# First attention layer: the products with V stand two steps behind the scores in place of one, with a third buffer of probabilities

## The reference, cut to what matters

```python
S = jnp.einsum('hid,hjd->hij', K, Q) * SCALE
delta = idx[:, None] - idx[None, :]
decay = jnp.where(delta < 0, 0.0, -delta.astype(jnp.float32) ** ALPHA)
S = jnp.where(delta < 0, -jnp.inf, S) + decay
C = jax.nn.softmax(S, axis=-1)
attn = jnp.einsum('hij,hjd->hid', C, V)
attn = attn.reshape(B, H, T, HD).transpose(0, 2, 1, 3).reshape(B, T, D)
return attn @ o_w.T + o_b
```

## Time and profile before

| | |
|---|---|
| median of 3 runs | 1562.99 us (1561.16 to 1569.36) |
| time of the profiled execution | 1574.49 us |
| its span, first to last instruction | 1572.8 us |
| PE, DVE, ACT busy over the span | 90%, 76%, 66% |
| first layer's attention | from 94 us to 546 us of the span |
| second layer's attention | from about 743 us to about 1390 us |

### The profile page before, as it was taken

The page is one execution under the profiler, slowest core; times in us unless marked ns, Lnnn a source line. Parts: engine busy times, 40 slices in busy tenths (PEclk is TensorE's granted clock), DMA queues, the critical chain, the costliest instruction groups (busy, mean ns, idle before and its releaser), DMA issues.

```text
span 1572.8 us, 35125 instructions
## 1 busy us (share of the span) xinstructions
PE 1423.1 (90%) x13272; PEld 601.4 (38%) x13272; DVE 1198.0 (76%) x1592; ACT 1034.1 (66%) x2043; POOL 308.0 (20%) x367
## 2 busy tenths in 40 slices
PE   7978798898999999986999999999999999998988
PEld 5643333333333354441233233333333333246664
DVE  5568797898786044788999979997999789536665
ACT  2135576777688833231799979988999889954432
POOL 1300122000000032223500038101200130154134
PEclk9888999999999999996999999999999999999999
DMA  7521120101000003223100200000000000012453
GB/s 226 124 54 41 35 80 27 37 27 49 5 2 2 1 14 68 48 48 92 49 7 8 54 5 6 7 7 6 7 7 6 7 2 2 19 64 85 142 154 119
DMA packets 57611, 68.54 MB, mean 44 GB/s; under 512 B 10563, under 2 KB 53123, under 8 KB 56707
## 3 DMA queue, kind: packets, MB, share of 16 engines
q1 hardware_dynamic: 54379, 57.90, 13.7%
q0 software_dynamic: 3072, 8.39, 1.8%
HBM read 45.29 MB, written 26.74 MB: 46 GB/s over the span
## 4 chain that ended last, share of the span: by engine, by line
PE 41%; issue 30%; DVE 16%; POOL 7%; ACT 5%; DMA 1%; another core or an unknown queue 0%; SPq 0%; POOLq 0%; DVEq 0%; ACTq 0%
DVE mpart L1704 13%; PE psum L1211 9%; PE psum L1186 5%; PE psum L1155 4%; ACT probs L1451 3%; PE psum L1328 3%; PE psum L1254 3%; PE psum L1282 2%; PE psum L1263 2%; PE psum L1347 2%; PE psum L1105 2%; PE psum L1241 1%; PE psum L1131 1%; PE psum L1319 1%; POOL ffn_w L937 1%
## 5 line engine op out<-in xcount | busy, mean ns | idle before, releaser
L1704 DVE TENSOR_REDUCE mpart<-psum 128x2 f32<-128x1024 f32 (+2 forms) x832 | 913.5, 1157 | 100.4 <-PE psum L1155 83.2
L1451 ACT ACTIVATE probs<-psum 128x512 f32<-128x512 f32 (+3 forms) x1664 | 846.4, 572 | 171.2 <-PE psum L1186 92.6
L1211 PE MATMUL psum<-probs,v_region 128*17 128x256 f32 (+2 forms) x6144 | 495.2, 395 | 11.7 <-ACT out_sb L1466 7.9
L1155 PE MATMUL psum<-key_region,row_region 50*128 50x512 f16 (+3 forms) x1664 | 322.7, 379 | 59.4 <-DVE mpart L1704 49.5
L1186 PE MATMUL psum<-row_region,key_region 52*128 52x512 f16 (+3 forms) x1664 | 348.9, 378 | 15.6 <-ACT probs L1451 13.4
L1186 PEld LDWEIGHTS psum<-row_region,key_region 52*128 52x128 f16 x1664 | 97.6, 93 | 352.1 <-ACT probs L1451 294.9
L1211 PEld LDWEIGHTS psum<-probs,v_region 128*17 128x17 f32 x6144 | 102.7, 95 | 206.2 <-issue 103.5
L1155 PEld LDWEIGHTS psum<-key_region,row_region 50*128 50x128 f16 x1664 | 94.4, 93 | 163.4 <-DVE mpart L1704 98.1
L899 POOL TENSOR_SCALAR vare<-mv 128x4 f32<-128x4 f32 x16 | 3.7, 232 | 635.3 <-DVE mv L1623 631.9
L1486 ACT ACTIVATE probs<-psum,gate_s 128x512 f32<-128x512 f32 (+1 forms) x24 | 16.4, 683 | 70.4 <-PE psum L1254 70.4
L1002 POOL TENSOR_TENSOR key_region<-probs,key_region 128x512 f16<-128x512 f32 (+1 forms) x24 | 27.9, 1166 | 153.7 <-ACT key_region L1495 153.6
(11 more groups left out here) (179 smaller groups left out, 1371.8 us busy)
## 6 DMA issues: line engine op xcount, KB each, us to landing
parts<-key_region SPq DMA_DIRECT2D x32, 256.0 KB, 2.8
key_region<-parts SPq DMA_DIRECT2D x48, 128.0 KB, 4.3
row_region<-parts SPq DMA_DIRECT2D x192, 32.0 KB
sorted_x<-in_zero SPq DMA_DIRECT2D x46, 128.0 KB, 2.6
key_region<-sorted_x SPq DMA_DIRECT2D x46, 128.0 KB
sorted_y<-key_region SPq DMA_DIRECT2D x46, 128.0 KB
key_region<-in_wmod SPq DMA_DIRECT2D x2, 1536.0 KB, 12.6
x_sb<-in_x SPq DMA_DIRECT2D x4, 512.0 KB, 8.3
```

What stands on the lines that cost most here:

```text
L1155: mm = pe.matmul(bank(b + par)[:, 0:w], rows[at, g, hp, r * P:(r + 1) * P], keys[at, g * HP + hp, q * CH:q * CH + w], start=True, stop=not ...
L1211: mm = pe.matmul(psum[32 * h:32 * h + VW, SUM_BANK, lo:hi], v_sb[:, jt, g * HG + h, :], probs[:, (S0[y] + s) % 2, h, lo:hi], start=(jt == ...
L1451: nc.scalar.activation(probs[:, (S0[y] + s) % 2, 2 * hp + par, off:CH], psum[:, e % 3, off:CH], ACT.Exp, scale=SCALES[y]).then_inc(s_p, 1)
L1704: V.tensor_reduce(mpart[:, n % NG, at:at + 2, q:q + 1], psum[:, b:b + 2, 0:w], AX.X, ALU.max).then_inc(drained(*item)[0], 1)
```

## The change

In the first layer, `values` of step s - 2 stands beside the scores of step s, where that of step s - 1 stood (`LAG = (2, 1)`: two for the first layer, one for the second, which keeps its order). A third buffer of probabilities lies in `ffn_w` behind the first layer's gate weights. `exps` waits for the products of three steps ago in place of two. All that follows the end of a unit (`oc`, `ft`, `bt`, `oq`, `op`, `st`, `nm`, `ln`) stands one step later, and `lh` at the first step of the unit after. At the end of the layer two steps of products are left in place of one. The maximum blocks, `mt`, `place`, `rows` and all DMAs stay where they are.

```diff
+LAG = (2, 1)
...
-            m, j = (n, k - 1) if k else (n - 1, steps_of(y, n - 1) - 1 if n else 0)
+            lag = LAG[y]
+            m, j = (n, k - lag) if k >= lag or not n else (n - 1, steps_of(y, n - 1) + k - lag)
             out.append(("sc", y, s, n, k, 0))
             out += work[:first]
-            if s:
-                out.append(("pv", y, s - 1, m, j, 0))
-            if n and n % NG == 0 and k == 3:
+            if s >= lag:
+                out.append(("pv", y, s - lag, m, j, 0))
+            if n and n % NG == 0 and k == lag + 2:
                 out.append(("oq", y, n // NG - 1))
             out.append(("sc", y, s, n, k, 1))
             out += work[first:second]
-            if s:
-                out.append(("pv", y, s - 1, m, j, 1))
-            if s and k == 0:
+            if s >= lag:
+                out.append(("pv", y, s - lag, m, j, 1))
+            if n and k == lag - 1:
                 out.append(("oc", y, n - 1))
...
-            if k == 1 and n:
+            if k == lag and n:
                 out.append(("ft", y, n - 1))
...
-                if k == 7:
+                if k == 7 and y:
                     out.append(("lh", 2 * y + 1, i))
...
+            if not y and k == 0 and n % NG == 1 and n > NG:
+                out.append(("lh", 1, n // NG - 1))
...
-    out += [("pv", y, total - 1, NU - 1, steps_of(y, NU - 1) - 1, z) for z in range(2)] + [("oc", y, NU - 1)]
+    out += [("pv", y, s, NU - 1, steps_of(y, NU - 1) + s - total, z) for s in range(total - LAG[y], total) for z in range(2)]
+    out.append(("oc", y, NU - 1))
...
+        prob_bufs = [probs[:, b, :, :] for b in range(2)] + [ffn_w[:, 0, KD * F0:KD * F0 + HG * CH].rearrange("p (h t) -> p h t", h=HG)]
...
+        def probs_of(y, s):
+            return prob_bufs[(S0[1] + s) % 2 if y else s % (LAG[0] + 1)]
...
-                if S0[y] + s >= 2 and hp == 0:
-                    act.wait_ge(s_pv, S0[y] + s - 1)
+                if hp == 0 and (y or s > LAG[0]):
+                    act.wait_ge(s_pv, S0[y] + s - LAG[y])
```

More of the change, by code:

```diff
@@ L201, in attention_walk @@
                 i = n // NG - 1
-                if k == 2:
+                if k == lag + 1:
                     out.append(("bt", y, i))
-                if k == 3:
+                if k == lag + 2:
                     out.append(("op", y, i))
-                if k == 4:
+                if k == lag + 3:
                     out.append(("st", 2 * y + 1, i))
-                if k == 5:
+                if k == lag + 4:
                     out.append(("nm", 2 * y + 1, i))
-                if k == 6:
+                if k == lag + 5:
                     out.append(("ln", 2 * y + 1, i))
-                if k == 7:
+                if k == 7 and y:
                     out.append(("lh", 2 * y + 1, i))
@@ L1211, in values @@
                         mm = pe.matmul(psum[32 * h:32 * h + VW, SUM_BANK, lo:hi], v_sb[:, jt, g * HG + h, :],
-                                       probs[:, (S0[y] + s) % 2, h, lo:hi], start=(jt == 0),
+                                       probs_of(y, s)[:, h, lo:hi], start=(jt == 0),
                                        stop=(z == 1 and jt == steps_of(y, n) - 1))
@@ L1450, in exps @@
                     act.wait_ge(s_e, e + 1)
-                    nc.scalar.activation(probs[:, (S0[y] + s) % 2, 2 * hp + par, off:CH], psum[:, e % 3, off:CH],
+                    nc.scalar.activation(probs_of(y, s)[:, 2 * hp + par, off:CH], psum[:, e % 3, off:CH],
                                          ACT.Exp, scale=SCALES[y]).then_inc(s_p, 1)
```

## The result

| kernel | median (range), us | runs |
|---|---|---|
| before | 1563.03 (1561.16 to 1569.36) | 7 |
| changed | 1572.89 (1570.92 to 1576.38) | 7 |

The ratio on record is 1.0047 [1.0025, 1.007], some 7 us slower; the two medians themselves lie 9.9 us apart. The forecast was 1562.0, and its range ended at 1569. Two later series with the same code gave 1.0000 [0.9975, 1.0025] and 1.0042 [1.0009, 1.0074]. So there are two things to explain, a loss and its coming and going.

A forecast was written before the change was run, and what follows sets the result against it. With maximum blocks DVE was taken as the bound, PE just behind; in the last 50 us ACT alone. Terms -2.0 - 0.5 + 0.5 + 0.5 + 0.6 = -0.9 us from 1562.99 gave 1562.1, stated as 1562.0, range 1554 to 1569.

The forecast's parts named there:

- The two wait terms: First layer's products with V wait less for probabilities: -2.0 us with maximum blocks, -0.5 in the last 50 us.
- The term of -2.0: First layer's stretch with maximum blocks: half the 3.9 us wait for probabilities gained (0 to -3.9).
- Narrow steps and unit starts: First layer's 16 units: PE's work is only redistributed between narrow and wide steps, +0.5 us.
- the middle: Over 16 units, +0.5 us between 5.0 lost if DVE or ACT paces wide steps and 4.0 gained if PE does.
- The prediction's own sign of it: First layer: forecast wrong if the count or length of stretches at clock 0.50 changes by more than 10 us.
- The rival in which the clock falls: Three of sixteen units fall to 1.2 GHz after two light opening steps: +9.3 us, 1572.3; chance 0.07.
- The end of the layer: After the first layer's last scores, one more half step of products on PE: +0.6 us (0.2 to 0.6).
- `lh`: Two ACT operations of 1.15 us move from a narrow step to unit 5's first wide one: +0.5 us.
- The third buffer: Third buffer of probabilities, with POOL writing the gate weights beside it: 0 us.

The follow-up runs named there:

- the fourth: Fourth series: the changed kernel without any addition, run a third time, against the kernel before: 1572.1 us for 1566.15, ratio 1.0042.
- The two splits: Kernel before with three buffers and lag 2 only in units 0 to 3 (ratios 1.004, 1.0036) or only in units 4 to 15 (1.000, 1.0008).
- the third series: The changed kernel without any addition, run once more against the kernel before: 1574.29 us, ratio 1.0000.

## Why the prediction was wrong, point by point

**The two wait terms (-2.0 and -0.5).** Their sum of -2.5 lies near the traces, -2.1 us in units 4 to 15, but not by the reasons given, and with an interval that holds 0 at equal time at the low clock. With maximum blocks DVE holds the step: its usual 2.23 us are the same in both kernels (units 13 and 14, step by step). The term of -2.0 is therefore not confirmed as a wait that was filled. For the last 50 us the prediction said "ACT alone is the bound there" and that the step would stay at 2.12 us. It fell to 2.01 in eight steps of unit 15, some -0.9 us in place of -0.5. The bound was a loop through ACT and PE, and when the lag opened it, PE's own 2.01 us were left. The unit as a whole gained nothing from it in the first pair of traces: its third step went from 2.09 to 4.77 us on PE, with a stretch at 0.50 that the kernel before did not have there, and its fifteen full steps took 32.9 us for 32.6. The gap that repeats on PE (the rule of the Trainium skill's page Perfetto Trace Analysis, Optimization Strategy) did mean a missing buffer here, worth 0.11 us a step and not the whole gap; the reading of ACT as saturated was the wrong one of the two.

**Narrow steps and unit starts (+0.5): this is the step that failed.** It was worked out as work that shifts between wide and narrow steps, "the middle" between a DVE-bound and a PE-bound case, over 16 like units. The units are not alike. In units 13 to 15 little of it was seen: the last narrow step takes 1.60 us on PE in both kernels (+0.09 was forecast), the third narrow one of unit 13 grew by 0.18, and the second step of unit 14 gave back 0.9 us that the two after it took again. In the first chunk a unit has only four steps, each narrower than the one before, PE waits for a transfer, and the lag takes work away from before the wait and puts it behind. That costs 1.3 us in unit 1 at full clock, and with what goes with the low clock the chunk is 3.2 us longer (±1.7) by the traces. By the timed runs lag 2 in the chunk alone costs 0.4%, some 6 us, of which 2.0 (±0.8) stand at equal clock. In place of +0.5 for sixteen units the first four alone had this, and the sum had nothing for it.

**The clock: the sum had no term.** This is the other half of the step that failed: the sum put a change of the time at 0.50 at nothing, and in the chunk it grew by 9.4 us (±5.8). The prediction's own sign of it, over 10 us more in the layer, came in the first trace (44.4 us for 30.6) and not in the two later ones of the same kernel (27.3 in both). The rival in which the clock falls had 0.07 and gave 1572.3, where 1572.9 was measured. In kind it was right, in its place and its price not. It had three of sixteen units fall behind two light steps. Behind the chunk that happened at two openings: in unit 15 a stretch at 0.50 stands in nine of nine traces with lag 2 there, and in five of eight without, and in unit 9 in four of nine and in none of eight. In exchange one in unit 12 and one in unit 8, each there in eight of eight with lag 1, were left in only two of nine. The rest as a whole had less of it, the first chunk more. It took half of a stretch as its price; measured are 0.26 us per us in the chunk. Light steps at each unit's start are not shown as the cause. Nor is the wait for the rows of unit 4: two of three traces of the changed kernel have it without a stretch in unit 1, taking it away left the stretches of units 0 and 3, and filling it did not bring time back. What keeps the clock low longer in units 0 and 3 stays open.

**Why 0, 6 or 7 us.** At equal clock the change costs +2.4 us (±0.9), and the traces have +0.8 (chunk) - 0.6 (rest) + 0.3 (end of the layer) = +0.5 (±1.9). They agree within their intervals and no better. On top comes the clock of the series: -0.0016 in the fourth is +1.8 us, +0.0022 in the third is -2.5 us and makes the ratio 1.0000. For the runs of the result itself the clocks of the kernel before aren't known; the changed kernel had 0.9627, lower than in either later series. The two splits had -0.0030 and -0.0028 with lag 2 in the chunk and nothing with lag 1 there, so in those two series the lower clock goes with the order. Why the third series shows the opposite stays open. Its ratio of 1.0000, near what was forecast, is then luck of the clock and no support for the sum.

**Smaller terms.** The end of the layer cost +0.3 us for +0.6 (range 0.2 to 0.6): the added product ran beneath the last exponentials. `lh` can't be read apart from the clock (the trace of unit 5 differs by more than its 1.15 us). The third buffer cost 0 as forecast, and the second layer is unchanged: in the traces its attention takes 645.9 us before and 646.1 after.

## What to carry to other kernels

A deeper lag pays where a step is a loop through two engines, and only down to the own work of the fuller one: here 0.11 us a step in the stretch without maximum blocks. It showed nothing where a third engine holds the slots. It must be worked out for the first, short rounds on their own: there the lag takes away the work that covers the first transfers. Where the clock moves in a kernel, compare at equal mean clock and repeat a series before believing 0.5%.

## What the runs showed of the hardware

- A run's time follows its mean granted clock, whichever kernel it is: -1.13 us per 0.001 within a series, correlation -0.8 to -0.98 for every kernel. A mean of 0.967 falls and rises between runs of the same code from 0.959 to 0.974, which is 17 us.
- A microsecond at clock 0.50 costs 0.26 us (±0.07) in the first chunk and 0.21 (±0.13) in units 4 to 15, about half of the 0.5 us that PE alone would lose at half its speed. The slope over whole runs comes to more, 0.36 (an estimate: 0.001 of 1570 us is 3.1 us at 0.50).
- An exponential of 128x512 lasts 0.60 us in a row by itself, and behind another one it starts 0.48 to 0.49 us after it. A block that is listed as one, at 0.53 to 0.54 apart on average, had hidden pauses, and so had the one at 0.503: to call an engine saturated, compare the distance from one start to the next with the shortest seen anywhere.
- The last stage, which no experiment touched, took 173 to 175 us in some series and 180 to 186 in others, most of the 10 us between their levels. The first of these is the changed kernel's, the second its repetition's:

```profile
1396.90:1570.30 173.40, 157.83 (x1194) 110.29 (x1194) 109.91 (x262) 67.33 (x173) 70.10 (x76) 0.98 0.40 123
```

```profile
1387.10:1567.20 180.10, 160.85 (x1194) 110.56 (x1194) 110.06 (x262) 66.68 (x173) 70.84 (x76) 0.97 0.39 118
```

PE was busy 3 us longer and idle 4 us longer; what it waited for was not traced further.
